# A router's sigmoid taken from silu on ScalarE instead of a power on GpSimd

## What is computed

```
x = x + attention(layernorm(x))        # linear attention: Q (K^T V), per batch of 2048 tokens
y = layernorm(x)
scores = sigmoid(y @ Wr)               # router: 8 experts
idx = top_k(scores + router_bias, 2)
w = scores[idx] / (sum + 1e-9)         # cw: w scattered to the 8 experts
routed = sum_{e<4} cw[e] * (silu(y Wg[e]) * (y Wu[e])) Wd[e]
routed += (cw[4] + cw[6]) * y + cw[7] * relu(y)
x = x + routed + conv4(y)              # depthwise causal convolution with 4 taps and a bias
```

## Time and profile before

| | value |
|---|---|
| median of three runs | 904.6 us (903.67 to 906.21) |
| the profiled execution | 902.03 us, of which the span from its first to its last instruction is 900.2 us |
| granted clock of TensorE, mean | 0.988 |
| PE busy | 865.2 us, 96% of the span |
| PE busy in 40 equal slices, tenths | 5789999999999999999999999999999999999997 |
| DVE busy | 701.8 us, 78% |
| DVE idle before `hidden` (L966) until a POOL gate product (L1273) ends | 59.0 us in 25 waits |
| ACT busy | 600.7 us, 67% |
| POOL busy | 565.3 us, 63%, of which enx (L1314) 177.7 us and the gate products (L1273) 166.2 us |
| chain that ended last | PE 86%, DVE 6%, POOL 3%, ACT 2%, issue 2% |

### The profile page before, as it was taken

The page is one execution under the profiler, slowest core; times in us unless marked ns, Lnnn a source line. Parts: engine busy times, 40 slices in busy tenths (PEclk is TensorE's granted clock), DMA queues, the critical chain, the costliest instruction groups (busy, mean ns, idle before and its releaser), DMA issues.

```text
span 900.2 us, 16555 instructions
## 1 busy us (share of the span) xinstructions
PE 865.2 (96%) x5402; PEld 765.8 (85%) x5402; DVE 701.8 (78%) x2030; ACT 600.7 (67%) x1212; POOL 565.3 (63%) x654
## 2 busy tenths in 40 slices
PE   5789999999999999999999999999999999999997
PEld 4668889898899988989889888998888898788876
DVE  5757878888778887788787887788878877777675
ACT  5675776777686677668567767666766765665553
POOL 3336776667676657667666767666666765566663
PEclk9989999999999999999999999999999999999999
DMA  9111434432434452343444243545324344344332
GB/s 285 56 53 42 138 121 141 135 104 84 127 118 141 143 138 72 101 136 118 142 141 112 76 120 118 142 141 142 109 66 132 95 117 118 95 117 110 103 90 74
DMA packets 79444, 103.84 MB, mean 115 GB/s; under 512 B 6528, under 2 KB 58880, under 8 KB 79360
## 3 DMA queue, kind: packets, MB, share of 16 engines
q1 hardware_dynamic: 74752, 86.02, 30.0%
q0 software_dynamic: 4608, 16.78, 9.9%
HBM read 68.96 MB, written 17.04 MB: 96 GB/s over the span
## 4 chain that ended last, share of the span: by engine, by line
PE 86%; DVE 6%; POOL 3%; ACT 2%; issue 2%; DMA 0%; POOLq 0%; DVEq 0%; ACTq 0%
PE ps_gu L394 12%; PE ps_gu L396 12%; PE ps_gu L395 12%; PE ps_y L394 6%; PE ps_gram L460 6%; PE ps_y L396 6%; PE ps_y L395 6%; PE ps_sh L512 6%; PE ps_sh L485 3%; PE ps_gram L462 3%; PE ps_sh L502 3%; PE ps_y L444 3%; PE ps_gu L535 2%; PE ps_gu L537 2%; PE ps_sh L561 2%
## 5 line engine op out<-in xcount | busy, mean ns | idle before, releaser
L1273 POOL TENSOR_TENSOR gate<-gate,cwb 128x512 f32<-128x512 f32 x128 | 166.2, 1298 | 135.3 <-ACT gate L728 128.0
L394 PE MATMUL ps_gu<-x2T_hi,wgu_hi 128*128 128x512 f32 x512 | 211.2, 413 | 0.1
L396 PE MATMUL ps_gu<-x2T_hi,wgu_lo 128*128 128x512 f32 x512 | 202.6, 396 | 0.0
L395 PE MATMUL ps_gu<-x2T_lo,wgu_hi 128*128 128x512 f32 x512 | 201.9, 394 | 0.0
L1314 POOL TENSOR_TENSOR enx<-inv_e,logits 128x32 f32<-128x32 f32 x32 | 177.7, 5552 | 9.0 <-ACT logits L721 9.0
L394 PE MATMUL ps_y<-wd_hi,hid_hi 128*128 128x256 f32 x512 | 153.3, 299 | 4.0 <-DVE hid_lo L973 3.1
L396 PE MATMUL ps_y<-wd_hi,hid_lo 128*128 128x256 f32 x512 | 145.5, 284 | 0.0
L395 PE MATMUL ps_y<-wd_lo,hid_hi 128*128 128x256 f32 x512 | 145.1, 283 | 0.0
L984 DVE SCALAR_TENSOR_TENSOR conv<-x2T,conv_w,conv 128x512 f32<-128x512 f32 x192 | 141.2, 773 | 0.0
L966 DVE TENSOR_TENSOR hid<-ps_gu,gate 128x512 f32<-128x512 f32 x128 | 86.0, 672 | 64.6 <-POOL gate L1273 59.0
L728 ACT ACTIVATE gate<-ps_gu 128x512 f32<-128x512 f32 x128 | 75.7, 592 | 65.3 <-PE ps_gu L396 65.2
(11 more groups left out here) (103 smaller groups left out, 1870.3 us busy)
## 6 DMA issues: line engine op xcount, KB each, us to landing
cwb<-cw_rows SPq DMA_DIRECT2D x128, 256.0 KB, 3.9
xa<-in_x SPq DMA_DIRECT2D x32, 512.0 KB, 7.9
acc<-in_x SPq DMA_DIRECT2D x32, 512.0 KB, 7.1
acc<-x POOLq DMA_DIRECT2D x32, 512.0 KB, 4.6
out<-acc SPq DMA_DIRECT2D x64, 256.0 KB, 2.7
cwb<-in_wg SPq DMA_DIRECT2D x4, 128.0 KB, 4.0
cwb<-in_wu SPq DMA_DIRECT2D x4, 128.0 KB, 3.8
cwb<-in_wd SPq DMA_DIRECT2D x1, 512.0 KB, 4.6
```

Of the source, the lines that this page charges most:

```text
L394: nc.tensor.matmul(dst, a_hi, b_hi, start=start, stop=False, skip_group_check=True)
L395: nc.tensor.matmul(dst, a_hi, b_lo, start=False, stop=False, skip_group_check=True)
L396: return nc.tensor.matmul(dst, a_lo, b_hi, start=False, stop=stop, skip_group_check=True)
L1273: g.tensor_tensor(gate[:, e % 2], gate[:, e % 2], cwb[:, q, e], ALU.mult).then_inc(gatew_ready, 1)
```

## The change

POOL's power is removed with its two constants, and so is the addition. In its place the sigmoid is put together from silu, which ScalarE uses for the experts already. With m = max(|logit|, 2^-100), silu(-m) = -m sigmoid(-m); divided by m this is minus the smaller of sigmoid and 1 - sigmoid (`minor`). Adding 1 where the logit is positive gives `signed`, and max(signed, -signed) is the score.

- ACT: `logits_copy` now issues two instructions, the copy and Abs into `size`; it waits for the cw of the group before instead of for enx. A new `score_dip` is the silu of -mag. In `body` it stands behind `hid_high(0)` and ahead of `silu(2)`; in the head right behind `logits_copy`.
- DVE: a new `magnitude` (max with 2^-100) stands behind `hidden(0)` and ahead of the third convolution tap. `route` starts with four instructions in place of one.
- DVE: in drain steps 34 to 37 `route` now stands directly behind `hidden(1)`, ahead of `hid_low(1)`, the residuals, the layernorm's statistics and `hidden(2)`. Before it stood behind `hidden(2)` in steps 34 to 36, and between `hid_low(1)` and `hidden(2)` in step 37. In all other steps it stays behind `hidden(2)`.
- PE: two waits for the logits now wait for both of ACT's reads of the bank.
- POOL: `power` is gone from the head and from `body`.

The core of the diff:

```diff
-        N_CONST = 8
+        N_CONST = 6
-        RT = 7 + 2 * TG
+        RT = 10 + 2 * TG
@@ PE: xn_transpose in the head; attention(st, 1)
-                        pe.wait_ge(logits_ready, 1)
+                        pe.wait_ge(logits_ready, 2)
...
-                    pe.wait_ge(logits_ready, st.before("R", 1, 1))
+                    pe.wait_ge(logits_ready, st.before("R", 2, 2))
@@ ACT
                 if st.later("R", 1):
-                    act.wait_ge(enx_ready, st.before("R"))
+                    act.wait_ge(cw_ready, st.before("R"))
                 copy(logits[:, :], ps_sh[0][:, 0:TG * NE]).then_inc(logits_ready, 1)
+                nc.scalar.activation(size[:, :], ps_sh[0][:, 0:TG * NE], ACT.Abs).then_inc(logits_ready, 1)
+
+            def score_dip(st):
+                act.wait_ge(mag_ready, st.before("R", 1, 1))
+                if st.later("R", 1):
+                    act.wait_ge(cw_ready, st.before("R"))
+                nc.scalar.activation(dip[:, :], mag[:, :], ACT.Silu, scale=-1.0).then_inc(dip_ready, 1)
@@ ACT body
                     hid_high(st, 0)
+                if r_on:
+                    score_dip(st)
                 if c_on:
                     silu(st, 2)
@@ DVE
+            def magnitude(st):
+                dve.wait_ge(logits_ready, st.before("R", 2, 2))
+                if st.later("R", 1):
+                    dve.wait_ge(dip_ready, st.before("R"))
+                v.tensor_scalar(mag[:, :], size[:, :], LEAST, None, ALU.max).then_inc(mag_ready, 1)
...
-                dve.wait_ge(den_ready, st.before("R", 1, 1))
-                done(v.reciprocal(flat(score[:, :, :]), den[:, :]))
+                dve.wait_ge(mag_ready, st.before("R", 1, 1))
+                done(v.reciprocal(rmag[:, :], mag[:, :]))
+                dve.wait_ge(dip_ready, st.before("R", 1, 1))
+                after()
+                done(v.tensor_tensor(minor[:, :], dip[:, :], rmag[:, :], ALU.mult))
+                after()
+                done(v.scalar_tensor_tensor(signed[:, :], logits[:, :], 0.0, minor[:, :], ALU.is_gt, ALU.add))
+                after()
+                done(v.scalar_tensor_tensor(flat(score[:, :, :]), signed[:, :], -1.0, signed[:, :], ALU.mult, ALU.max))
@@ DVE body
                     hidden(st, 0)
+                if r_on:
+                    magnitude(st)
+                if c_on:
                     conv_tap(st, 2)
...
+                if r_on and (drain or not b_on):
+                    route(st)
                 if c_on:
                     hid_low(st, 1)
                 if b_on and drain:
                     residual(st, 0)
                     residual(st, 1)
                     norm2_stats(st)
-                if r_on and c_on and not b_on:
-                    route(st)
                 if c_on:
                     hidden(st, 2)
-                if r_on and c_on and b_on:
+                if r_on and b_on and not drain:
                     route(st)
@@ POOL
-            def power(st):
-                pool.wait_ge(logits_ready, st.before("R", 1, 1))
-                g.tensor_tensor(enx[:, :], inv_e[:, :], logits[:, :], ALU.pow).then_inc(enx_ready, 1)
...
-                g.tensor_tensor(den[:, :], enx[:, :], one_e[:, :], ALU.add).then_inc(den_ready, 1)
```

More of the change, by code:

```diff
@@ L40 @@
 TAKEN = -2.0e38
+LEAST = 2.0 ** -100
 class Step:
@@ L149, in program @@
         ident = sb("ident", [P, P])
-        one_e = sb("one_e", [P, TG * NE])
         eps_ln = sb("eps_ln", [P, TG])
@@ L153, in program @@
         half_neg = sb("half_neg", [P, TG])
-        inv_e = sb("inv_e", [P, TG * NE])
         xa = sb("xa", [P, 4, TG, H])
@@ L185, in program @@
         logits = sb("logits", [P, TG * NE])
-        enx = sb("enx", [P, TG * NE])
-        den = sb("den", [P, TG * NE])
+        size = sb("size", [P, TG * NE])
+        mag = sb("mag", [P, TG * NE])
+        dip = sb("dip", [P, TG * NE])
+        rmag = sb("rmag", [P, TG * NE])
+        minor = sb("minor", [P, TG * NE])
+        signed = sb("signed", [P, TG * NE])
         score = sb("score", [P, TG, NE])
@@ L273, in program @@
         logits_ready = sem("logits_ready")
-        enx_ready = sem("enx_ready")
-        den_ready = sem("den_ready")
+        mag_ready = sem("mag_ready")
+        dip_ready = sem("dip_ready")
         rt = sem("rt")
@@ L871, in head @@
                 logits_copy(r)
+                score_dip(r)
                 xnT_high(at("A", 2, NG), 0)
@@ L1159, in head @@
                 x2T_low(r, 1)
+                magnitude(r)
                 xnT_low(at("A", 2, NG), 0)
@@ L1240, in _ @@
             g.memset(two8[:, :, :], ABSENT).then_inc(const_ready, 1)
-            g.memset(one_e[:, :], 1.0).then_inc(const_ready, 1)
             g.memset(half_neg[:, :], -0.5).then_inc(const_ready, 1)
-            g.memset(inv_e[:, :], math.exp(-1.0)).then_inc(const_ready, 1)
             g.memset(eps_ln[:, :], EPS_LN).then_inc(const_ready, 1)
@@ L1310, in skip_factors @@
                 g.tensor_tensor(skip_scale[:, q], coef_rstd[:, :], ones4[:, :], ALU.add).then_inc(skip_ready, 1)
-            def power(st):
-                pool.wait_ge(logits_ready, st.before("R", 1, 1))
-                g.tensor_tensor(enx[:, :], inv_e[:, :], logits[:, :], ALU.pow).then_inc(enx_ready, 1)
-                pool.wait_ge(enx_ready, st.before("R", 1, 1))
-                if st.later("R", 1):
-                    pool.wait_ge(rt, st.before("R", RT, 1 - RT))
-                g.tensor_tensor(den[:, :], enx[:, :], one_e[:, :], ALU.add).then_inc(den_ready, 1)
             def head():
@@ L1324, in head @@
                 norm2_factors(at("B", 1, NG))
-                power(at("R", 0, NG))
                 skip_factors(at("R", 0, NG))
@@ L1332, in body @@
                     gate_weight(st, 1)
-                if r_on:
-                    power(st)
                 if c_on:
```

## The result

The changed kernel took 901.25 us (median of 17 runs, 897.51 to 904.12), the kernel before 904.0 (17 runs, 901.33 to 907.92). The ratio is 0.9967, 95% interval [0.9952, 0.9982], about 3.0 us. The bound of 0.3%, on which the forecast stood, lies inside the interval. What is steady in this and what isn't is half of what follows.

A forecast was written before the change was run, and what follows sets the result against it. PE was taken as the bound, 96% busy, with its waits in the tail from step 34. Terms 0.3 + 0 - 0.4 + 0.1 - 2.8 = -2.8 took the median from 904.6 to 901.8 us; range 900.5 to 903, with rivals 898.8 to 906.0.

The forecast's parts named there:

- The bound of 0.3%: Whole run: a change within 0.3%, 2.7 us, can't be told from none; the line for faster is 901.9.
- Power and addition off POOL: Steps 8 to 32: removing 64 POOL instructions is worth nothing, since PE's own stream covers them.
- mag in the repeating steps: DVE ahead of the third convolution tap: mag takes 0.10 of 0.12 free, cost 0; bounds 0 and 14 us.
- The head, +0.3: Head: table load and silu behind the logits delay xnT_hi, for which PE waits; +0.3, bounds 0 and 1.5.
- the fifth rival: Head: a drain of about 1.38 us adds to the table load, losing 1.7, not 0.3; 903.2 us, chance 0.04.
- Step 33, -0.4: Step 33: PE's 0.54 wait for the first residual shrinks by 0.4; hid_low(2) stays behind ACT's hid_hi(2).
- Steps 34 to 36, +0.1: Drain steps: POOL's product holds one routing instruction, 1.04 lost; the wait moves from cw to hid_lo(2); +0.05 a step.
- the first rival: Steps 34 to 36: the new route meets no product, 1.1 less each, step 36's clock fall goes; 897.1, chance 0.14.
- Step 37, -2.8: Step 37: 0.85 lost ahead of down 1, down 2 starts 1.4 earlier, the clock's 1.4 saved; bounds 0 and -3.7.
- The clock: Rival: one-piece 2.0 us waits bring falls in steps 34, 35 and still 37, 1.4 each; 906.0, chance 0.14.

The follow-up runs named there:

- the two comparisons: Changed kernel against the kernel before, on two chips: 901.25 against 904.0 us, ratio 0.9967; then 901.07 against 900.38 us, ratio 1.0003.
- e7: Changed kernel with the magnitude's operation four times instead of once in the repeating steps: ratio 1.0004 to the kernel before.
- e9: Changed kernel with the magnitude's operation eight times instead of once in the repeating steps: 905.66 us, ratio 1.0062 to the kernel before.
- e5: Changed kernel with GpSimd's gate product 2 waiting for hid_lo(1) in steps 34 to 36: 896.61 us, ratio 0.996 to the kernel before.
- e6: Changed kernel, steps 34 to 36: product 2 waits for hid_lo(1); hidden(2), product 3, hid_hi(3) precede second-norm work: 894.51 us, ratio 0.9932 to kernel before.
- e1: Changed kernel with the routing of steps 34 to 37 at its old places, new sigmoid only: 909.34 us, ratio 1.0065 to the kernel before.
- e3: Changed kernel with the routing moved in steps 34 to 36 alone, not in 37: 901.56 us, ratio 0.9975 to the kernel before.
- e4: Kernel before with the routing at its new places, POOL keeping its power: 913.01 us, ratio 1.0108 to the kernel before.

## Why the prediction was right, and which steps were not

The forecast was 901.8 us, the result 901.25, inside the forecast's own range. The change was forecast at -2.8, half of it waiting and half clock; the work part shows -1.1 and -1.2 of waiting in the two comparisons, and the clock came out once as forecast and once the other way. Point by point:

- *Power and addition off POOL, worth nothing in the repeating steps*: right, the routers of steps 8 to 32 keep their distance.
- *mag in the repeating steps, 0 by a hair*: 0 is right, the hair is not. The tap ends at 418.10 and PEld takes it at 418.21, so by the load 0.05 is left, as the step had it. But PE's matmul comes 0.23 after the load. The room is about 0.25, shown by e7 (at its edge, 0.03 a step lost) and e9 (beyond).
- *The head, +0.3*: wrong, 0. ACT did what the step said, xnT_hi at 48.12, which is 0.27 later than 48.01 less the common shift of 0.16:

```profile
46.39 0.20 ACT L724 ACTIVATE logits<-ps_sh 128x32 f32<-128x32 f32 x1 [1.54 <-PE ps_sh L515]
46.48 0.19 ACT L831 ACTIVATE size<-ps_sh 128x32 f32<-128x32 f32 x1
46.69 1.28 ACT L838 ACT_TABLE_LOAD   x1
47.99 0.23 ACT L838 ACTIVATE dip<-mag 128x32 f32<-128x32 f32 x1
48.12 0.58 ACT L724 ACTIVATE xnT_hi<-ps_sh 128x512 fp32r<-128x512 f32 x1
```

  The next router stands at 68.43, before at 68.60: the same shift as at the start, so nothing is left of the 0.27. The step failed in taking a delay of a producer for one of PE at the next place where PE waits. The drain of the fifth rival isn't there either: ACT was busy until 46.67, the load starts 0.02 later, takes 1.28, and the silu follows 0.02 behind it. The Trainium skill (ScalarE: Activation LUTs, What ACT_TABLE_LOAD costs) has a drain of about 1.38 on top; this trace doesn't agree.
- *Step 33, -0.4*: wrong, 0. PE still waits 0.54 for the first residual (775.08). hidden(2) did move up, from 769.00 to 768.54, and stopped at PE's gate_up 5. But the new route is 0.74 longer from its reciprocal to `biased`, which then stands 0.3 later than before, and the sum's epsilon is held by gate product 3, before and after. That product waits for ACT and starts where it did (771.96, before 772.01), so the end of the routing stays where it was. The prediction took ACT's hid_hi(2) for the limit; it ends at 772.34, and hid_lo(2) starts at 773.64, behind the routing. Its step left out the length of the new route and the hold, both of which it had for steps 34 to 36. DVE, then POOL:

```profile
768.54 0.69 DVE L980 TENSOR_TENSOR hid<-ps_gu,gate 128x512 f32<-128x512 f32 x1 [1.17 <-PE ps_gu L399]
...
772.36 0.93 DVE L1081 TENSOR_SCALAR wsum_eps<-wsum 128x4 f32<-128x4 f32 x1
...
771.96 1.30 POOL L1302 TENSOR_TENSOR gate<-gate,cwb 128x512 f32<-128x512 f32 x1 [5.14 <-ACT gate L731]
```

- *Steps 34 to 36, +0.1*: the mechanism is right in each part, the place of the held operation too (`biased`), and step 35 came out at 23.53 against 23.51 (e9 has 23.54 and 23.57 in steps 34 and 35). Step 34 of this trace took 0.6 less, because the product met only the short copy `two`, held 0.5 instead of 1.0: part of the first rival, in one step of three, and brought about by the fall of the clock ahead of it. e5 shows the hold itself, e6 what the kernel can do without it.
- *Step 37, -2.8*: right in this pair of traces, 1.3 of stall and 1.4 of clock; PE's wait ahead of down 1 is 0.69 where 0.85 was forecast. e1 to e3 show that the sigmoid earns it. The stall is steady; the 1.4 of clock is there to be saved only in executions in which the kernel before has that fall.
- *The clock*: I had one fall behind the new pauses as a rival and none in the forecast. In the profiled execution one went (step 36) and one came, at a place I hadn't looked at: the 1.07 wait for the transposes ahead of router 34.

The sum: forecast 0.3 + 0 - 0.4 + 0.1 - 2.8; trace 0 + 0 + 0 + 0 - 2.7, plus 1.6 - 0.6 for the fall ahead of step 34 and its consequence, less 1.5 for the fall that is gone in step 36: -3.2. That the two terms that were wrong, +0.3 and -0.4, nearly cancel is luck. So is it that the clock's half came out as forecast: on the other chip it did not, and nothing was left of the gain.

What stays open: why the kernel before has a clock part of 9.8 us on one chip and 13.0 on another while the changed kernel's is 11.6 to 11.8. On the chip with 9.8, 13 of the 29 executions of the kernel before list a mean clock of 0.992, a clock part of 7.2 us, where the execution whose trace is read here has 0.988 and 10.8. The difference of 3.6 is that of two falls or a little more, so in these 13 the falls behind the stalls of steps 36 and 37 were probably absent; none of the changed kernel's twelve executions there reached 0.992. That is an estimate: the kernel before was not traced on that chip. That the change itself makes falls less or more frequent is not shown.

## What to carry to other kernels

Before pricing a new wait, ask which operation of another engine will run beside the moved ones: here a product on GpSimd cost the routing 1.0 us in nearly every drain step. Delaying that product was worth 1.1 us of the work part, about as much as the change it was found by, and with the new order 3.8. A moved block pays only together with what makes its input early; tried alone, each half here was slower than none. A comparison of 0.3% should list the clock beside the time: span times granted clock separated 1.2 us of work, which repeated, from 9 to 16 us of clock, which did not. And before a shorter step in one trace is put down to a change, look whether the clock fell ahead of it.

## What the runs showed of the hardware that was not expected

- The same pause of PE is followed by a fall of the clock in one execution and not in another. In steps 34 to 36 of twelve traces (the kernel before, the changed one and ten experiments): pauses of 2.99 to 3.09 us, 6 falls in 6; 3.5 in two pieces, 2 in 3; 1.80 to 1.84, 4 in 13; 1.64 in two pieces, 1 in 3; 0.3 to 1.17, none in 11. But the pause of 1.07 ahead of router 34, 5.7 us behind one of 0.54, was followed by a fall in 3 of 12 traces: length alone doesn't decide. One fall costs about 1.5 us. A longer one, at 0.50 from 450 to 456 in e9's repeating steps, cost 3.1 and had no pause of PE of 0.1 us or more in the 25 us ahead of it.
- A held DVE operation need not be large: one of 128x32 elements with two operands in SBUF stood 1.0 us beside a 128x512 product on GpSimd, and so did a copy of 128x8 (1.25 us in e1). The residual adds, which read one operand in PSUM, and the statistics kept their length beside it (in e5 1.28 and 1.41 us, product from 821.15 to 822.45), and the 128x32 reciprocal took its usual 0.35 beside one in e4 (819.23, product from 819.15). POOL's powers held nothing: in the changed kernel hid_lo(2) took 0.69 at 824.86, beside the small one (128x4) from 824.19 to 825.22, and in the kernel before hid_lo(1) took 0.69 at 815.50, inside the 5.44 us of the large one that began at 811.29.
- PE's weight loads for the convolution ran 0.23 us ahead of its matmuls in the repeating steps (418.21 and 418.44 in the changed kernel); in e7 the load came 0.2 us late, cost at most 0.03 a step and was made up (8 loads in 0.86 us, not 1.02).
